# A graph layer on one core: eight message buffers, earlier loads of x, and one-hots made from a slot table that holds each edge's node

## The reference

```python
h = jnp.concatenate([x[row], x[col]], axis=-1)              # row = src, col = dst
msgs = jax.nn.silu(h @ W1.T + b1) @ W2.T + b2
agg = jax.ops.segment_sum(msgs, row, num_segments=n_nodes)
cnt = jax.ops.segment_sum(ones, row, num_segments=n_nodes)
agg = agg / (cnt + 1e-08)
gi = agg @ w_ih.T + b_ih;  gh = x @ w_hh.T + b_hh
r = sigmoid(i_r + h_r);  z = sigmoid(i_z + h_z);  n = tanh(i_n + r * h_n)
x_new = (1.0 - z) * n + z * x
y = gamma * (x_new - mean) / sqrt(var + 1e-05) + beta
out = layernorm(x + y)
```

## Time and profile before

| | |
|---|---|
| median of 3 runs | 2405.72 us |
| the profiled execution | 2403.31 us |
| its span, first to last instruction | 2401.6 us |
| PE busy | 2185.4 us (91%) |
| DVE busy | 1999.3 us (83%) |
| POOL busy | 1742.8 us (73%) |
| ACT busy | 1539.8 us (64%) |
| moved by transfers | 528.22 MB, mean 220 GB/s |

### The profile page before, as it was taken

One profiled execution on the slowest core, in us unless ns is written; L12 is line 12 of the kernel. 1 busy time (PEld: TensorE's weight loads), 2 busy tenths in 40 slices (PEclk: granted clock), 3 DMA queues, 4 the chain that ended last, 5 costly groups with the idle time before them and its releaser, 6 DMA issues.

```text
span 2401.6 us, 48711 instructions
## 1 busy us (share of the span) xinstructions
PE 2185.4 (91%) x10620; PEld 1667.8 (69%) x10620; DVE 1999.3 (83%) x6515; ACT 1539.8 (64%) x3158; POOL 1742.8 (73%) x1824
## 2 busy tenths in 40 slices
PE   6898998899898989889999999999999999999995
PEld 4777777777777777666666666676676667666763
DVE  6776776667676666669999999999999999999998
ACT  3444444444444444558888888888888888887876
POOL 5656666666666656468888888888888888888885
PEclk9999999999999999989999999999999999999998
DMA  5666666666566656657767677666666676766763
GB/s 159 219 222 211 217 231 211 219 211 227 207 230 217 215 202 215 225 198 227 237 232 227 227 235 238 228 236 222 228 231 228 230 235 226 239 232 224 234 215 131
DMA packets 206647, 528.22 MB, mean 220 GB/s; under 512 B 58696, under 2 KB 67680, under 8 KB 206608
## 3 DMA queue, kind: packets, MB, share of 16 engines
q1 hardware_dynamic: 124168, 320.62, 38.3%
q0 software_dynamic: 81600, 206.79, 26.9%
q10 hardware_dynamic: 840, 0.40, 0.1%
HBM read 475.46 MB, written 207.08 MB: 284 GB/s over the span
## 4 chain that ended last, share of the span: by engine, by line
PE 26%; DVE 24%; issue 19%; DMA 12%; POOL 8%; another core or an unknown queue 7%; ACT 2%; DVEq 1%; POOLq 0%; SPq 0%; ACTq 0%
PE banks L1086 23%; DMA mg<-messages,rows_now 11%; DVE tg L1028 4%; POOL mg L391 4%; DVE st L1064 3%; DVE uu L1039 3%; PE banks L1102 3%; DVE diff L1011 3%; DVE oh L990 2%; DVE zd L1016 2%; POOL xb L515 1%; DVE msg L779 1%; DMA xts<-in_xt 1%; POOL rs L531 1%
## 5 line engine op out<-in xcount | busy, mean ns | idle before, releaser
L1086 PE MATMUL banks<-whh,xts 128*128 128x512 f32 (+1 forms) x1568 | 561.5, 486 | 0.0
L391 POOL DMA_INDIRECT mg<-messages,rows_now x392 | 449.9, 1148 | 94.4 <-issue 86.0
L1086 PE MATMUL banks<-mg,oh 128*128 128x512 f32 (+1 forms) x1568 | 322.4, 348 | 78.3 <-DVE npre L1005 50.3
L587 ACT ACTIVATE msg<-banks 128x512 fp32r<-128x512 f32 (+1 forms) x392 | 187.0, 493 | 321.6 <-PE banks L1086 174.9
L1086 PEld LDWEIGHTS banks<-mg,oh 128*128 128x128 f32 x1568 | 253.3, 189 | 182.9 <-issue 128.1
L1086 PEld LDWEIGHTS banks<-whh,xts 128*128 128x128 f32 x1568 | 269.4, 189 | 151.8 <-issue 141.4
L391 POOL DMA_INDIRECT xsrc<-in_x,src_now x196 | 192.1, 980 | 243.4 <-PE banks L1102 113.6
L1086 PE MATMUL banks<-wsh,silh 128*128 128x512 f32 (+1 forms) x784 | 278.7, 356 | 80.8 <-DVE msg L779 77.2
L658 ACT ACTIVATE banks<-banks,rcount 128x768 f32<-128x768 f32 x392 | 326.5, 871 | 27.9 <-PE banks L1086 16.6
L779 DVE TENSOR_TENSOR msg<-banks,msg 128x512 fp32r<-128x512 f32 (+1 forms) x392 | 203.9, 552 | 163.5 <-ACT msg L587 129.1
L1086 PE MATMUL banks<-wsl,silh 128*128 128x512 f32 (+1 forms) x784 | 273.8, 349 | 0.0
(11 more groups left out here) (139 smaller groups left out, 5495.4 us busy)
## 6 DMA issues: line engine op xcount, KB each, us to landing
messages<-msg SPq DMA_DIRECT2D x196, 772.0 KB
xts<-in_xt SPq DMA_DIRECT2D x196, 256.0 KB
xs<-in_x SPq DMA_DIRECT2D x196, 256.0 KB
out_y<-yy SPq DMA_DIRECT2D x196, 256.0 KB
near<-tile_blocks SPq DMA_DIRECT2D x49, 128.0 KB
mg<-messages,rows_now POOLq DMA_INDIRECT x392
xsrc<-in_x,src_now POOLq DMA_INDIRECT x196
xdst<-in_x,dst_now POOLq DMA_INDIRECT x196
```

Source lines behind the costliest of these rows:

```text
L391: nc.gpsimd.indirect_dma_start(out=dst_tile, out_offset=None, in_=rows, in_offset=bass.IndirectOffsetOnAxis(ap=table, axis=0), bounds_chec ...
L587: nc.scalar.activation(msg[:, u % EU, n0:n1], p_g[:, part, 0:n1 - n0], ACT.Copy).then_inc(e_gh[part], 1)
L1086: return nc.tensor.matmul(out_, lhsT, rhs, start=start, stop=stop, skip_group_check=skip)
```

## The change

- `EU` goes from 4 to 8 message buffers. Buffers of the edge stage are laid out in another order to make room.
- `xs` and `xts` get `XQ = UNROLL = 8` buffers. SP loads `xts` for pair s + 5 and `xs` for pair s + 4. So that it doesn't run further ahead, each load also waits for the segment sum of five pairs earlier (`AHEAD = 5`).
- The number that an edge puts into the slot table is its row times 256 plus its node. After the table is read back, DVE splits it into `slot_row` (shifted right by 8) and `slot_node` (the low 8 bits, as fp32). An empty slot has node 0, which no entry of `iota1` (1 to 128) equals, so `slot_used` isn't needed.
- The one-hots of both blocks of a pair are one comparison of `iota1` with two columns of `slot_node`. It doesn't read `mg`; the wait for the gathers moves from DVE to PE's `segment_sum`.
- `copy_rows` waits for the landing of the gathers that used its columns, in place of DVE's `oh`.
- The semaphores of the two gathers of an edge tile are one, those of the two silu instructions are one, and those of the two gathers of a pair are one.

```diff
-EU = 4
+EU = 8
+XQ = UNROLL
+NODE_BITS = 8
...
-        got_x, got_xt, got_m, n_stored = sems("got_x", QU), sems("got_xt", QU), sems("got_m", 2 * QU), sems("n_stored", QU)
+        got_x, got_xt, got_m, n_stored = sems("got_x", XQ), sems("got_xt", XQ), sems("got_m", QU), sems("n_stored", QU)
...
             def load_x(q, u):
-                need(sp, S["n_xl"], q - QU + 1)
-                need(sp, S["n_mm"], q - QU + 1)
+                need_apart(sp, sp_passed, S["n_sg1"], q - AHEAD + 1)
+                need(sp, S["n_xl"], q - XQ + 1)
+                need(sp, S["n_mm"], q - XQ + 1)
             def load_rows(q, u):
-                need(sp, S["n_diff"], q - QU + 1)
-                need(sp, S["n_xb"], q - QU + 1)
+                need_apart(sp, sp_passed, S["n_sg1"], q - AHEAD + 1)
+                need(sp, S["n_diff"], q - XQ + 1)
+                need(sp, S["n_xb"], q - XQ + 1)
...
-            node_turns(sp, ((store_y, -8), (load_counts, 3), (load_x, 3), (load_rows, 2)), first=-4, last=8)
+            node_turns(sp, ((store_y, -8), (load_counts, 3), (load_x, 5), (load_rows, 4)), first=-5, last=8)
...
-            pool.wait_ge(st_got, 16)
+            pool.wait_ge(tab_ready, 1)
...
                 def copy_rows(q, u):
-                        need(pool, S["n_oh"], q - QU + 2)
+                        if not isinstance(q, int) or q >= QU:
+                            pool.wait_ge(got_m[u % QU], 32 * nth(q, u))
+                            pool.wait_ge(got_m[u % QU + 1], 32 * nth(q, u))
...
             def edge_message_hi(g, u, part):
-                need(act, e_stored[u % EU], 16 * quad(g, u))
+                need(act, e_stored[u % EU], 16 * g)
...
                 if n == TILES + 7:
                     dve.wait_ge(st_got, 16)
-                    nc.vector.tensor_scalar(slot_used[:, :], slot_row[:, :], float(EDGES_PAD), None, ALU.is_lt)\
+                    nc.vector.tensor_scalar(slot_low[:, :], slot_row[:, :], (1 << NODE_BITS) - 1, None, ALU.bitwise_and)\
+                        .then_inc(tab_step, 1)
+                    nc.vector.tensor_scalar(slot_row[:, :], slot_row[:, :], NODE_BITS, None, ALU.arith_shift_right)\
                         .then_inc(tab_ready, 1)
+                    dve.wait_ge(tab_step, 1)
+                    nc.vector.tensor_copy(slot_node[:, :], slot_low[:, :]).then_inc(tab_step, 1)
...
             def one_hot(q, u):
-                for h in range(2):
-                    need(dve, S[f"n_sg{h}"], q - QU + 1)
-                    dve.wait_ge(got_m[2 * u + h], 16 * (nth(q, u) + 1))
-                    last = nc.vector.tensor_scalar(oh[0:SLOTS, u, h, :], iota1[0:SLOTS, :],
-                                                   mg[0:SLOTS, u, h, LOC:LOC + 1].bitcast(f32),
-                                                   slot_used[0:SLOTS, bass.ds(q * 2 + h, 1)], ALU.is_equal, ALU.mult)
-                last.then_inc(S["n_oh"], 1)
+                need(dve, S["n_sg1"], q - QU + 1)
+                of = slot_node[0:SLOTS, bass.ds(q * 2, 2)].rearrange("p (h a) -> p h a", a=1)
+                nc.vector.tensor_tensor(oh[0:SLOTS, u % QU, :, :], iota1[0:SLOTS, :].rearrange("p (a l) -> p a l", a=1)
+                                        .to_broadcast([SLOTS, 2, P]), of.to_broadcast([SLOTS, 2, P]), ALU.is_equal)\
+                    .then_inc(S["n_oh"], 1)
...
             def segment_sum(q, u):
                 pe.wait_ge(S["n_oh"], q + 1)
-                pe.wait_ge(got_c[u], 16 * (nth(q, u) + 1))
+                pe.wait_ge(got_m[u % QU], 32 * (nth(q, u) + 1))
+                pe.wait_ge(got_c[u % QU], 16 * (nth(q, u) + 1))
```

More of the change, by code:

```diff
@@ L120, in gnn_layer @@
         count_rows = sb("count_rows", [P, 4, 2, P], until=early)
-        slot_bits, slot_parts = sb("slot_bits", [P, 3, BLOCKS], i32, until=early), sb("slot_parts", [P, 4, BLOCKS], until=early)
+        silh, sill = (sb(n, [P, 2, KC, SPAN], f32r, until=early) for n in ("silh", "sill"))
+        wsh, wsl = sb("wsh", [P, KC, G3], f32r, until=early), sb("wsl", [P, KC, G3], f32r, until=early)
         eh, el = (sb(n, [P, 2, 2 * KC, SPAN], f32r, until=early) for n in ("eh", "el"))
@@ L149, in gnn_layer @@
         setup.close()
+        apart = ExitStack()
+        sb("rows_below", [P, EU - 2, ROW], until=apart)
+        before, put = sb("before", [P, ROW], f32r, until=apart), sb("put", [P, ROW], f32r, until=apart)
+        apart.close()
+        general = ExitStack()
+        slot_bits, slot_parts = sb("slot_bits", [P, 3, BLOCKS], i32, until=general), sb("slot_parts", [P, 4, BLOCKS], until=general)
+        general.close()
         msg = sb("msg", [P, EU, ROW], f32r, until=early)
         early.close()
-        xs, xts = sb("xs", [P, QU, 2 * D]), sb("xts", [P, QU, 2 * D])
-        xb, xn = sb("xb", [P, QU, 2 * D]), sb("xn", [P, QU, 2 * D])
-        nt, diff, zd = (sb(n, [P, 2, 2 * D]) for n in ("nt", "diff", "zd"))
+        xs, xts = sb("xs", [P, XQ, 2 * D]), sb("xts", [P, XQ, 2 * D])
+        xb = sb("xb", [P, QU, 2 * D])
+        oh = sb("oh", [P, QU, 2, P], f32r)
+        nt = sb("nt", [P, 2, 2 * D])
         mg = sb("mg", [P, QU, 2, ROW], f32r)
-        oh = sb("oh", [P, QU, 2, P], f32r)
+        xn = sb("xn", [P, QU, 2 * D])
+        diff, zd = (sb(n, [P, 2, 2 * D]) for n in ("diff", "zd"))
         rz = sb("rz", [P, 2, 2, 2 * D])
@@ L245, in edge_slots, with nth @@
                     also(n)
-        def nth(q, u):
-            return (q if isinstance(q, int) else q - u) // QU + (0 if isinstance(q, int) else u // QU)
+        def nth(q, u, buffers=QU):
+            return q // buffers if isinstance(q, int) else (q - u) // buffers + u // buffers
         def duo(q, u):
@@ L576, in edge_silu @@
                 need(act, e_sl[m], k)
-                nc.scalar.activation(sil[:, m, :], p_hid[:, m, :], ACT.Silu, bias=b1s[:, m:m + 1]).then_inc(e_sil[m], 1)
+                nc.scalar.activation(sil[:, m, :], p_hid[:, m, :], ACT.Silu, bias=b1s[:, m:m + 1]).then_inc(e_sh[m], 1)
                 need(act, e_g[1], k * QUAD - QUAD)
@@ L638, in x_hi @@
             def x_hi(q, u):
-                act.wait_ge(got_xt[u], 16 * (nth(q, u) + 1))
+                act.wait_ge(got_xt[u], 16 * (nth(q, u, XQ) + 1))
                 need(act, S["n_mm"], q - QU + 1)
-                nc.scalar.activation(xh[:, u, :], xts[:, u, D:2 * D], ACT.Copy).then_inc(S["n_xh"], 1)
+                nc.scalar.activation(xh[:, u % QU, :], xts[:, u, D:2 * D], ACT.Copy).then_inc(S["n_xh"], 1)
             def gates(q, u, h):
@@ L710, in _ @@
             dve.wait_ge(idx_ready, N_IDX)
+            nc.vector.scalar_tensor_tensor(out=place_row[:, 1, :], in0=cst[:, C_ROW:C_ROW + TILES], scalar=float(1 << NODE_BITS),
+                                           in1=locf[:, :], op0=ALU.mult, op1=ALU.add).then_inc(st_empty, 1)
             dve.wait_ge(w1_hi, 1)
@@ L921, in _ @@
             with dve.If(n_levels > 1):
+                for u in range(EU):
+                    dve.wait_ge(e_stored[u], 16 * len(range(u, TILES, EU)))
                 nc.vector.memset(put[:, :].bitcast(f32), 0.0).then_inc(v_zero, 1)
```

116 lines of the change are left out of this document (57 added, 59 removed).

## The result

The changed kernel took 2339.03 us (median of 4 runs, 2331.87 to 2345.99), the kernel before 2404.81 us (4 runs, 2399.23 to 2411.65). The ratio is 0.9725, with a 95% interval of 0.9684 to 0.9766. 2345 us were predicted, in a range of 2322 to 2382.

What follows compares the result with a forecast made beforehand. DVE was taken to bound the node stage and PE's chain the edge stage. From the profiled 2403.3 us, 30.5 (landing) and 33 (comparison) off and 3 (between stages) on gave 2342.8, as a median 2345 us, range 2322 to 2382.

Steps and rivals of the forecast that it cites:

- DVE bounds the stage, PE's own turn is 6.32 us: Node stage: DVE sets the 6.85 us turn, since PE waits for its `npre`; PE alone could turn in 6.32 us.
- The turn: Node stage: each turn falls from 6.85 to 6.52 us, by 0.16 us of waiting and 0.17 us of comparison.
- The landing leaves DVE, 30.5 us: Node stage: DVE's 33 waits for gathers vanish and PE does not wait instead; 30.5 us gained, bounds 0 and 33.
- Earlier loads of x ... I take nothing: Node stage: ending ACT's 12 waits for `xts` gains nothing, as ACT has time to spare; bounds 0 and 6 us.
- cover of 3.35 us: Node stage: a gather may land up to 3.35 us after the moment that releases DVE today without PE waiting.
- One comparison in place of two, 33 us: DVE's one-hots, node stage: 0.34 us replaces 0.51, saving 0.17 us in each of 196 turns, 33 us.
- Between the stages, +3 us: Between edge and node stage: 1 us of POOL delay from table operations, 2 us from two more x loads before the gathers.
- Eight buffers, copy_rows, semaphores: 0: Eight message buffers, `copy_rows`' new wait and merged semaphores: nothing; `copy_rows` 0 to 3 us, semaphores 5 us, either way.
- The pair at its old cost: Rival, DVE in node stage: the broadcast comparison takes 0.51 us like the old two, so 2378 us; chance 0.08.
- The landing back on PE: Rival, node stage: gathers land over 3.35 us later, PE waits where DVE did, 30.5 us stay, 2375 us; chance 0.08.
- DVE held by POOL: Rival, node stage: the comparison waits for POOL's `rs`, 0.98 us every second turn, so 2441 us, slower; chance 0.06.
- The edge stage: Rival, edge stage: PE's 80 us of stalls came from the buffers, so 98 us more gain, 2247 us; chance 0.03.

Runs made afterwards that it cites:

- compare_twice: Changed kernel with its 256-column comparison made a second time, into a tile nobody reads; 2268.36 us, 0.9991 of the kernel before.
- pe_three_more: Changed kernel with three more matmuls of 256 columns on PE in each turn, so outputs differ; 2236.48 us, 0.9835 of the kernel before.
- x_as_before: Changed kernel with x in four buffers, loaded three and two turns ahead, without the new gate; 2209.92 us, 0.9724 of the kernel before.
- two_scalars: Changed kernel with two 128-column comparisons, each with two scalars per partition, no wait for gathered rows; 2385.61 us, 0.9864 of the kernel before.
- two_compares: Changed kernel with two 128-column comparisons, each with one scalar per partition and constant 1.0; 2215.38 us, 0.9753 of the kernel before.
- four_buffers: Changed kernel with four message buffers in use, the tile keeping its size for eight; 2203.05 us, 0.9695 of the kernel before.
- all_three: Changed kernel with two-scalar comparisons, DVE's wait for gathered rows and the late x loads all back; 2423.38 us, 1.0008 of the kernel before.
- after_again: The changed kernel once more, unaltered, as control; 2205.19 us, 0.9709 of the kernel before.

## Why the prediction was right, and which step of it failed

*DVE bounds the stage, PE's own turn is 6.32 us.* Right, and shown from both sides by compare_twice and pe_three_more.

*The turn.* 6.52 us were predicted and 6.52 came; 63.5 us for the stage, and 64.3 came.

*The landing leaves DVE, 30.5 us.* The sum was right: the wait went whole and did not come back on PE. The mechanism is shown to suffice: with the x loads as before, and the rows as late, DVE's not waiting still keeps all but 3 to 7 us. What failed is the term beside it, "Earlier loads of x ... I take nothing". The runs show two parts that each suffice: with DVE waiting as before, the early loads alone keep all but 2 us. That one term stood for the wait and the other at nothing came out right in the sum by luck, as the two overlap whole. The prediction expected of the new loads that they "can delay a gather"; they made it quicker, by 0.9 to 1.0 us at the median and 1.7 to 2.2 at the 95th per cent. It looked at the volume and ACT's wait, and not at which transfers are issued on top of a gather. Its cover of 3.35 us was also read too large: before 1640.56 PE had itself waited 1.81 us for `npre`, which DVE, held by that same gather, made late. Without that wait 1.5 us are left. x_as_before has 1.55 at the least, so it was enough.

*One comparison in place of two, 33 us.* The size was right: 0.336 us to the next start against an estimate of 0.34, and 37 us for the pair in two_scalars. The reason given is right in its first half, "most of each is a fixed part", and incomplete in its second, "the change pays it once": most of the gain is that the new comparison has no scalars. 256 more columns cost the tensor-tensor comparison 0.602 - 0.336 = 0.27 us, 1.04 ns a column, which leaves 0.07 us for an instruction. Two tensor-scalar operations of the edge stage, with one scalar per partition each and issued one behind the other, show the other form's price (DVE's timeline of the changed kernel):

```profile
44.30 0.61 DVE L888 TENSOR_SCALAR total<-bias_c,cst 128x768 f32<-128x768 f32 x1
44.83 0.35 DVE L890 TENSOR_SCALAR before<-before,cst 128x256 f32<-128x256 f32 x1
45.10 0.56 DVE L753 SCALAR_TENSOR_TENSOR picked<-banks,ohb 128x392 f16<-128x392 f32 x1
```

To the next start they take 0.529 and 0.263 us (to the ns in the trace, and the same within 2 ns in all 14 traces), so 512 columns cost 0.27 us, 0.52 ns a column, and 0.13 us are fixed. By that, 128 columns with one scalar take 0.07 + 0.13 = 0.20 us, and two_compares has 0.196; the second scalar adds 0.06 (two_scalars). `ve`, two columns and no such scalar, takes 0.07, so the first costs about 0.06 too. As an estimate, then: of the old pair's 0.51 us, 0.24 were scalars, 0.14 the two instructions and 0.13 columns. The new one pays 0.07 once and no scalar, but 0.27 for the columns. The Trainium skill (VectorE: DVE Perf Modes, the perf-mode tier table) lets an fp32 tensor-scalar operation from SBUF run at twice the rate of a tensor-tensor one, and these rows agree. The prediction set that rule aside with "the trace doesn't bear it out"; the loss of 0.13 us a turn was real, and hidden behind the 0.24 of the scalars, of which it had no term. So the size came out right without its parts.

*Between the stages, +3 us.* Nearly nothing came: PE's wait rose by 0.2 us. The first table operation costs what `slot_used` did. POOL's last conversion ended at 1011.55, the second operation, for which POOL waits, at 1012.04, and POOL's copy came 4.69 us after that; before, it came 1022.58 - 1017.96 = 4.62 us after the conversions. So POOL was held for 0.5 us, where 1 was taken. The two more loads, put at 2 us, did not delay the first gathers.

*Eight buffers, copy_rows, semaphores: 0.* Right (four_buffers, all_three).

*The rivals.* The pair at its old cost: `tg` starts 0.33 us after it, not 0.51. The landing back on PE: no such wait. DVE held by POOL: in 92 turns the comparison started inside POOL's `rs`, and took 0.417 us by mean and 0.421 at most, as ever (POOL's timeline, then DVE's):

```profile
1614.11 1.37 POOL L542 TENSOR_TENSOR rs<-ve,halves 128x4 f32<-128x4 f32 x1
...
1614.49 0.42 DVE L1018 TENSOR_TENSOR oh<-iota,slot_node 126x256 fp32r<-126x256 f32 x1
```

The rule that the Trainium skill has for this pair (SBUF — State Buffer, who interferes with whom) doesn't show in these rows. The first table operation, another form, did stretch: 3.15 us beside POOL's conversions, where the second took 0.35 without them. The edge stage: its buffers bring nothing; the 6 us that it was shorter lie within the scatter below.

## What to carry to other kernels

Read an operation's price on a bounding engine from start to start, and count its scalars, and the rate of its form, as well as its columns: here a second scalar per partition was worth more than merging two instructions (27 us against 10). Where an engine waits for a transfer, ask both who could wait in its place and what is issued on top of that transfer; undo the two apart and together, since either may be enough, and then each looks worthless alone. A sum can come out right with a term given to one edit alone that two edits each bring, or with two costs of opposite sign left out.

## What the runs showed that was not expected

The same program took 2339 us in one set of runs and 2205 in another, and the kernel before 2405 and 2269. The difference lies in the edge stage: it ended at about 1006 us in the first trace and at 878 in after_again; from the first to the last `npre` the two took 1272.1 and 1272.9 us. The windows and waits of the edge stage, first of the first trace of the changed kernel, then of after_again:

```profile
100.00:850.00 750.00, 674.76 (x3628) 556.64 (x3626) 525.37 (x1890) 318.07 (x603) 473.78 (x567) 0.97 0.64 219
```

```profile
ACT msg L607 <- PE banks L1113: 128.9, 87, 3.5
POOL xsrc L408 <- remote: 86.3, 48, 2.4
ACT msg L607 <- remote: 84.5, 51, 5.2
```

```profile
100.00:850.00 750.00, 750.00 (x4221) 634.93 (x4220) 609.91 (x2199) 389.31 (x703) 543.19 (x649) 1.00 0.72 254
```

```profile
ACT msg L607 <- PE banks L1113: 191.1, 88, 2.2
```

In the slower trace PE stands 75 of 750 us, with waits of up to 5.2 us whose releaser the profile can't name, and the clock is granted at 0.97. In the quicker one PE never stands, no such wait exists, and the clock is 1.00. In the slower traces increments of semaphores by PE often arrive 1 to 3 us after the instruction's end (for the step of PE where it is most frequent, made once in each tile, 110 of 170 recorded increments of the first trace are over 0.3 us late, for four other steps 56 to 72 of 144 to 176 are; in after_again none is). What makes them late stays open. The prediction's last rival looked for the cause of PE's 80 us of stalls in the kernel's buffers; with the same code and the same buffers they can be absent.
